# The cross-attention block's input fed a second time, transposed: centred Wq and rstd as the scale of the exponential in place of transposes of x

## The reference, cut to what matters

```python
def layernorm(x): return (x - mean(x)) / sqrt(var(x) + 1e-5)          # over D = 256
# x: (2, 1024, 256); context: (2, 64, 256); 16 heads of 64; 8 experts, top 2, F = 1024
q = layernorm(x) @ Wq;  k = context @ Wk * 64**-0.5;  v = context @ Wv
attn = softmax(q k^T);  x = x + tanh(g_xattn) * ((attn v) @ Wo + bo)
seq = layernorm(x).mean(axis=1);  probs = softmax(seq @ gate_w)       # top 2 experts per batch
x = x + tanh(g_ffn) * sum_e share_e * (gelu(layernorm(x) @ w1[e] + b1[e]) @ w2[e] + b2[e])
```

## Time and profile before

| | |
|---|---|
| median of 3 runs | 323.07 us (323.06 to 323.4) |
| the profiled execution | 322.94 us, of which the span of its instructions is 320.8 us |
| busy | PE 314.4, DVE 233.7, ACT 164.1, POOL 78.8 us |
| attention steps 0 to 16 | about 17 to 131 us of the span |

### The profile page before, as it was taken

How to read it: one execution, slowest core, us unless ns; L and a number is a source line. 1 busy time by engine, 2 the same in 40 slices (tenths; PEclk the granted TensorE clock), 3 DMA queues, 4 the chain that set the end, 5 groups by cost and what they waited for, 6 DMA issues and landing times.

```text
span 320.8 us, 5745 instructions
## 1 busy us (share of the span) xinstructions
PE 314.4 (98%) x1881; PEld 272.1 (85%) x1881; DVE 233.7 (73%) x563; ACT 164.1 (51%) x577; POOL 78.8 (25%) x158
## 2 busy tenths in 40 slices
PE   7899999999999999999999999999999999999996
PEld 7887988988999999988788888888887899888896
DVE  1889997978889999999998475466667554442643
ACT  2548555686766668775466254444533442321320
POOL 1325448484455536335600000000000000000000
PEclk9999999999999999999999999999999999999999
DMA  6992000000000017600007250000020000000011
GB/s 224 395 197 4 2 3 0 0 3 3 0 0 3 0 52 246 230 1 0 2 0 263 55 208 1 0 0 0 8 102 24 2 0 2 0 0 0 2 65 65
DMA packets 20765, 17.35 MB, mean 54 GB/s; under 512 B 11068, under 2 KB 16900, under 8 KB 20612
## 3 DMA queue, kind: packets, MB, share of 16 engines
q1 hardware_dynamic: 20464, 16.51, 17.0%
q10 hardware_dynamic: 276, 0.52, 0.5%
HBM read 14.93 MB, written 2.10 MB: 53 GB/s over the span
## 4 chain that ended last, share of the span: by engine, by line
PE 88%; DVE 7%; DMA 2%; issue 1%; ACT 1%; SPq 0%; DVEq 0%
PE ps L1098 26%; PE ps L1100 26%; PE ps L1099 26%; PE ps L1183 4%; DMA xt<-in_x_dram 2%; PE ps L1272 1%; PE ps L1118 1%; DVE mx L850 1%; PE ps L1156 1%; DVE pT_lo L808 1%; PE ps L1214 1%; PE ps L1370 1%; ACT sx L580 1%; DVE stats L729 1%; DVE sm L819 1%
## 5 line engine op out<-in xcount | busy, mean ns | idle before, releaser
L667 ACT ACTIVATE gel<-ps,b1sel 128x512 f32<-128x512 f32 x64 | 43.9, 690 | 95.5 <-PE ps L1100 95.4
L1057 DVE CAST h_hi<-gel 128x512 fp32r<-128x512 f32 x64 | 28.4, 443 | 58.7 <-ACT gel L667 58.5
L580 ACT ACTIVATE sx<-ps,mx 128x64 f32<-128x64 f32 x128 | 38.3, 327 | 27.6 <-DVE mx L850 27.6
L1098 PE MATMUL ps<-yT_hi,w_hi 128*128 128x512 f32 (+1 forms) x128 | 50.5, 395 | 0.0
L1099 PE MATMUL ps<-yT_lo,w_hi 128*128 128x512 f32 (+1 forms) x128 | 50.0, 390 | 0.0
L1100 PE MATMUL ps<-yT_hi,w_lo 128*128 128x512 f32 (+1 forms) x128 | 49.9, 390 | 0.0
L1059 DVE TENSOR_TENSOR h_lo<-gel,h_hi 128x512 fp32r<-128x512 f32 x64 | 44.9, 702 | 2.2
L466 POOL TENSOR_TENSOR sx<-sx,rs 128x512 f32<-128x512 f32 x32 | 33.2, 1058 | 48.0 <-DVE rs L824 47.8
L1098 PE MATMUL ps<-h_hi,w_hi 128*128 128x512 f32 x96 | 38.4, 400 | 0.0
L1100 PE MATMUL ps<-h_hi,w_lo 128*128 128x512 f32 x96 | 37.5, 390 | 0.0
L1099 PE MATMUL ps<-h_lo,w_hi 128*128 128x512 f32 x96 | 37.4, 390 | 0.0
(11 more groups left out here) (145 smaller groups left out, 672.7 us busy)
## 6 DMA issues: line engine op xcount, KB each, us to landing
stage_w<-in_L_ffn_w_dram SPq DMA_DIRECT2D x7, 1024.0 KB, 7.3
out_dram<-xt SPq DMA_DIRECT2D x6, 256.0 KB, 2.5
wqT<-in_L_xattn_Wq_dram SPq DMA_DIRECT2D x2, 512.0 KB, 7.9
wv_sb<-in_L_xattn_Wv_dram SPq DMA_DIRECT2D x2, 512.0 KB, 9.3
wo_sb<-in_L_xattn_Wo_dram SPq DMA_DIRECT2D x1, 1024.0 KB, 13.7
xt<-in_x_dram SPq DMA_DIRECT2D x1, 1024.0 KB, 10.7
stage_w<-in_L_ffn_w_dram SPq DMA_DIRECT2D x2, 512.0 KB, 4.4
wk_sb<-in_L_xattn_Wk_dram ACTq DMA_DIRECT2D x1, 512.0 KB, 4.2
```

Of the source, the lines that this page charges most:

```text
L580: last = nc.scalar.activation(sx[:, par, c0:c0 + M], ps[:, 2 * par + 1, c0 - BANK:c0 - BANK + M], ACT.Exp, bias=mx[:, par, h:h + 1], accum ...
L667: nc.scalar.activation(gel[:, f % 4, :], ps[:, h_bank, :], ACT.Gelu, bias=b1sel[:, b, slot, f:f + 1]).then_inc(gelu_done, 1)
L1057: nc.vector.tensor_copy(h_hi[:, f % 4, :], gel[:, f % 4, :]).then_inc(hhi_ready, 1)
L1098: mm(acc, hi_w, hi_x, start=start, stop=False)
```

## The change

The launch gets x a second time, laid out on the host as `xT` (partition = feature). Scores are now made from the raw transposed x. The mean is taken out by centring Wq over the feature axis (its row sums are removed on the chip before `score_pair`), and rstd is applied as the scale of the exponential, with the maxima of the last eight heads multiplied by it (`mxs`).

```diff
@@ SP: the loads
+            def load_xT(i):
+                t0, t1 = XT_LOADS[i]
+                part = 0 if t0 < XS0 else 1 if t0 < XS1 else 2
+                base = (0, XS0, XS1)[part]
+                sp.dma_start(xs[part][:, t0 - base:t1 - base, :, :], xT[:, t0:t1, :, :]).then_inc(ld_xT[i], 16)
...
-            load_x(1, 0, 2, TB // 2)
...
+            load_x(0, 0, 0, TB // 2)
+            load_xT(0)
...
+            sp.wait_ge(grp_done, number[("kT", 1)] + 1)
+            load_xT(2)
+            load_xT(3)
@@ POOL
-                t = s + LEAD
-                if active(t) and t != X_BY_DVE:
...
-                    nc.gpsimd.tensor_tensor(xn[:, par, :], tile, mean1[:, ds(t, 1)].broadcast_to([P, D]),
-                                            ALU.subtract).then_inc(xc_ready, 1)
...
-                if s == 1:
-                    newton(*X_PARTS[1], rstd1, ve_x, 2)
-                    pool.sem_inc(x_rstd, 1)
-                if s == 4:
-                    newton(*X_PARTS[2], rstd1, ve_x, 3)
-            pool.wait_ge(guess_ready, 1)
+                if active(s + LEAD):
+                    x_low(s + LEAD)
+                if s in (-1, 3, 6):
+                    x_rstds((-1, 3, 6).index(s))
...
+            def x_low(t):
+
+                pool.wait_ge(xhi_ready, t + 1)
+                nc.gpsimd.tensor_tensor(xT_lo[:, t % XB, :, :], x_raw(t), as_f32(xT_hi[:, t % XB, :, :]),
+                                        ALU.subtract).then_inc(xlo_ready, 1)
+
+            for half in range(2):
+                pool.wait_ge(wq_mean, half + 1)
+                for m in range(4 * half + 2, 4 * half + 4):
+                    last = nc.gpsimd.tensor_tensor(wqT[:, m, :], wqT[:, m, :], wq_off[:, m:m + 1].broadcast_to([P, D]), ALU.add)
+                last.then_inc(wq_pool, 1)
@@ ACT
+            def wq_centred(half):
+
+                act.wait_ge(wq_mean, half + 1)
+                for m in range(4 * half, 4 * half + 2):
+                    last = nc.scalar.activation(wqT[:, m, :], wqT[:, m, :], ACT.Identity, bias=wq_off[:, m:m + 1])
+                last.then_inc(wq_act, 1)
 
             group("kT", 0)
+            wq_centred(0)
             group("kT", 1)
+            wq_centred(1)
...
-                act.wait_ge(max_done, t + 1)
+                act.wait_ge(mxs_ready, t + 1)
...
-                                                ACT.Exp, bias=mx[:, par, h:h + 1],
+                                                ACT.Exp, bias=mxs[:, par, h - H // 2:h - H // 2 + 1],
+                                                scale=rstd1[:, t:t + 1],
@@ DVE
+            def wq_means(half):
+
+                blocks = slice(4 * half, 4 * half + 4)
+                dve.wait_ge(ld_wq[half], 16)
+                nc.vector.tensor_reduce(wq_off[:, blocks], wqT[:, blocks, :], AX, ALU.add).then_inc(wq_sum, 1)
+                dve.wait_ge(wq_sum, half + 1)
+                nc.vector.tensor_scalar(wq_off[:, blocks], wq_off[:, blocks], -1.0 / D, None, ALU.mult).then_inc(wq_mean, 1)
...
-            x_norm(0)
+            for half in range(2):
+                wq_means(half)
+            x_stats(0, range(0, TB // 2))
...
+            for g in A0[:4]:
                 group(*g)
-            x_low(0)
-            for g in A0[6:]:
+            x_norm(0)
+            for g in A0[4:]:
                 group(*g)
...
-                if s == 4:
-                    x_norm(2)
...
+                    dve.wait_ge(x_rstd, next(i for i, (t0, t1) in enumerate(X_PARTS) if t < t1) + 1)
+                    nc.vector.tensor_scalar(mxs[:, par, :], mx[:, par, H // 2:H], rstd1[:, t:t + 1], None,
+                                            ALU.mult).then_inc(mxs_ready, 1)
...
-                    x_norm(1)
...
-                if s in (2, 3):
-                    x_stats(3, range(TB + 4 * (s - 2), TB + 4 * (s - 2) + 4))
+                if s == 2:
+                    x_stats(1, range(TB // 2, TB))
+                    x_norm(1)
+                if s in (3, 4):
+                    x_stats(2, range(TB + 4 * (s - 3), TB + 4 * (s - 3) + 4))
+                if s == 5:
+                    x_norm(2)
@@ PE
-                pe.wait_ge(ld_wq[half], 16)
+                pe.wait_ge(wq_act, half + 1)
+                pe.wait_ge(wq_pool, half + 1)
...
-                    for k in range(KD):
-                        last = nc.tensor.transpose(ps[:, 7, k * P:(k + 1) * P], xn[:, q, k * P:(k + 1) * P], ident[:, :])
-                    last.then_inc(xT_done, 1)
```

More of the change, by code:

```diff
@@ L75, in gated_cross_attention_moe_kernel @@
     mx = place("mx", [P, 2, H])
+    mxs = place("mxs", [P, 2, H // 2])
     sm = place("sm", [P, 2, H])
@@ L114, in gated_cross_attention_moe_kernel @@
     ctxT = place("ctxT", [P, KD, P], at=first)
+    XS0, XS1 = 6, 14
+    xs = [place("xs0", [P, XS0, KD, P], at=first),
+          place("xs1", [P, XS1 - XS0, KD, P], at=[cursor[0]])]
     first2 = [cursor[0]]
@@ L138, in gated_cross_attention_moe_kernel @@
     pT_lo = place("pT_lo", [P, 2, NP, P], f32r, at=second)
-    xT_hi = place("xT_hi", [P, 2, KD, P], f32r, at=second)
-    xT_lo = place("xT_lo", [P, 2, KD, P], f32r, at=second)
-    xn = place("xn", [P, 2, D], at=second)
+    XB = 3
+    xT_hi = place("xT_hi", [P, XB, KD, P], f32r, at=second)
+    xT_lo = place("xT_lo", [P, XB, KD, P], f32r, at=second)
     yT_hi = place("yT_hi", [P, KD, NT * P], f32r, at=second)
@@ L169, in gated_cross_attention_moe_kernel @@
         ld_wk = [sem(f"ld_wk_{i}") for i in range(2)]
-        ld_x = [sem(f"ld_x_{i}") for i in range(4)]
+        ld_x = [sem(f"ld_x_{i}") for i in range(3)]
         ld_g, ld_bo, ld_gate, ld_b12 = sem("ld_g"), sem("ld_bo"), sem("ld_gate"), sem("ld_b12")
@@ L182, in gated_cross_attention_moe_kernel @@
         ln_ready, xc_ready = sem("ln_ready"), sem("xc_ready")
[L183 to L184 removed]
+        xhi_ready, xlo_ready = (sem(n) for n in ("xhi_ready", "xlo_ready"))
+        ld_xT = [sem(f"ld_xT_{i}") for i in range(4)]
+        wq_sum, wq_mean, wq_act, wq_pool = (sem(n) for n in ("wq_sum", "wq_mean", "wq_act", "wq_pool"))
+        mxs_ready = sem("mxs_ready")
         scores_done, head_done, max_done, sub_done, exp_done, sum_done, recip_done, mul_done = (
@@ L329, in gated_cross_attention_moe_kernel, with x_raw, wait_x_raw @@
         X_PARTS = [(0, TB // 2), (TB // 2, TB), (TB, NT)]
-        X_BY_DVE = X_PARTS[1][0]
+        XT_LOADS = [(0, 2), (2, XS0), (XS0, XS1), (XS1, NT)]
+        def x_raw(t):
+            part = 0 if t < XS0 else 1 if t < XS1 else 2
+            return xs[part][:, t - (0, XS0, XS1)[part], :, :]
+        def wait_x_raw(eng, t):
+            eng.wait_ge(ld_xT[next(i for i, (t0, t1) in enumerate(XT_LOADS) if t < t1)], 16)
         def run_steps(step):
@@ L833, in step @@
                         group(*g)
-                t = s + 1
-                if active(t) and t >= 2:
-                    q = (par + 1) % 2
-                    if s in Y_WITH_X:
-                        dve.wait_ge(yhi_ready, Y_WITH_X[s] + 1)
-                    dve.wait_ge(xhi_ready, t + 1)
-                    nc.vector.tensor_tensor(xT_lo[:, q, :, :], ps[:, 7, 0:D].rearrange("p (k i) -> p k i", k=KD),
-                                            as_f32(xT_hi[:, q, :, :]), ALU.subtract).then_inc(xlo_ready, 1)
                 if s in Y_WITH_X:
@@ L1431, in _laid_out @@
         a = a.T.reshape(-1, 128, a.shape[0]).transpose(1, 0, 2)
+    if name == "xT":
+        b, s, d = a.shape
+        a = a.reshape(b, 128, s // 128, d // 128, 128).transpose(4, 0, 2, 3, 1)
+        a = a.reshape(128, b * s // 128, d // 128, 128)
     return _np.ascontiguousarray(a)
```

96 lines of the change are left out of this document (39 added, 57 removed).

## The result

The changed kernel takes 341.87 us in the median (340.89 to 342.61, four runs) against 323.06 us (322.88 to 323.4) before: ratio 1.058, 95% interval 1.0549 to 1.0609. I had said 323.7 and at most 325.2. The profiled execution took 340.89 us, its span is 339.0. The granted clock of TensorE is 1.0 in both profiled executions, so the 18.2 us between their spans have to be found in waits and lengths. Single executions in a slower state of the chip are left out of all medians and ratios.

The account below looks back on a forecast made before the run. PE was taken to bound the kernel from about step 5 on, DVE and ACT before that. +1.9 us (POOL's new wait) - 1.3 us (steps 9 to 14) = +0.6 us on a median of 323.07 gave 323.7 us, range 322.1 to 325.2.

Parts of the forecast that it names:

- steps 1 to 6: Early attention steps, paced by DVE and ACT: one xT_lo (0.28 us) less, mxs (0.2 us) more, rounds nearly alike.
- Transposes: PE, steps 1 to 14: one pair of xn transposes less per step, 0.22 us each, at most 3.1 us.
- Steps 9 to 14: PE sets the pace again; six pairs of xn transposes less give -1.3 us.
- The start: Before the first scores: centring Wq makes PE start A one us later; mx(0) at 20.9 us, +0.4 us.
- The clock rival: The start: PE's gap before A halves its clock, 1.5 us more, late Wq another us; 324.7 to 326.2 us, chance 0.13.
- recip(5) at 61.8: DVE's reciprocal of tile 5, 61.74 us before, comes at 61.8, between 61.2 and 63.0.
- scores(8) at 75.1: PE's score matmul of step 8 begins at 75.1 us instead of 73.24, +1.9 us.
- POOL's new wait: Steps 6 to 8: two Newton blocks of 3.87 us in a row delay mul(6), and PE waits; +1.9 us.
- the first rival: Transposes pay in full, POOL's blocks not holding up mul(6): -1.6 to -2.8 us, 320.3 to 321.5 us; chance 0.12.
- The sum: Whole kernel: +1.9 - 1.3 = +0.6 us, predicting 323.7 us.
- The second rival: Half is hidden, recip(5) coming a us or more earlier: -0.3 to -1.1 us, 322.0 to 322.9 us; chance 0.15.

Follow-up runs that it names:

- e4_before_scale: The kernel before with a column of ones added as scale in the nine exponentials of a step; 332.28 us (1.0287).
- e3_neither: The changed kernel without the scale operand in the exponentials and without the product of the maxima (`mxs`); 324.74 us (1.0047).
- e1_no_scale: The changed kernel with the scale operand taken out of the exponentials, the product of the maxima kept; 332.47 us (1.028).
- e2_no_mxs: The changed kernel without the product of the maxima, the exponentials taking the unscaled maxima as bias; 331.40 us (1.0254).
- e7_act_mxs: The changed kernel with the product of the maxima made by ACT instead of DVE, ahead of the exponentials; 335.87 us (1.0379).
- e8_no_max: The changed kernel with the maxima left out of the softmax, two exponentials of 128x512 with scale per step; 324.22 us (1.0044).
- e5_neither_newton5: e3_neither with the third rstd (Newton) block on POOL moved from step 6 to step 5; 320.47 us (0.9916).

## Why the prediction was wrong

The step that failed is the one on steps 1 to 6, "So rounds of before and after are nearly alike", in two terms. The product of the maxima stood there "above a whole xT_lo of 0.28; I take 0.2": it takes 0.69 us in the mean, and without it 10.5 us come back. The scale of the exponentials was not costed at all, though it is an operand added to nine instructions per step, eight of which stand one behind the other on the loop: 9.4 us come back without it. I had drawn the loop rightly, and had named, as what would make me wrong, that DVE and ACT become the pace from step 9 on; but I gave it no chance and no price. The margin was thin, and I had not worked it out: PE's rounds were 6.95 us. Those of ACT and DVE follow only from `e4_before_scale`, where they set the pace at 7.6 to 7.7 us: 7.65 - 0.83 = 6.8 us, so that some 0.2 us more per round was enough. The Trainium skill, in ScalarE: Activation LUTs, under "What ACT_TABLE_LOAD costs", puts each operand with one value per partition (a pointer operand) at about 93 ns more. The traces nearly agree: exponentials 81 to 83 ns longer, whose starts lie 95 ns further apart. By the page's figure nine operands are 0.84 us per round, an estimate, beside the 0.83 measured.

The other steps, read in the run with neither (`e3_neither`), where PE sets the pace as I had assumed:

- *Transposes.* 0.22 us for a pair. Rounds of 6.72, 6.72, 6.77 and 6.74 us behind scores(8), where the kernel before has 6.95, 6.92, 6.95 and 6.95: right. In the changed kernel itself they are removed and bring nothing.
- *Steps 9 to 14, -1.3 us.* From scores(8) to scores(15) 123.03 - 75.46 = 47.57 against 122.16 - 73.24 = 48.92 us: -1.35, right.
- *The start, mx(0) at 20.9.* It came at 21.45 in the changed kernel and 21.8 here: +0.95 to +1.3 instead of +0.4. In the changed kernel DVE's sums started at 8.22 and A at 11.05, half a us before my 11.6; what I had too short was the way from there, where two operations of the guess take 0.60 and 0.66 us beside POOL's `xT_lo`:

```profile
15.59 0.16 DVE L758 TENSOR_SCALAR ve_x<-ve_x 128x4 f32<-128x4 f32 x1
15.63 1.42 POOL L500 TENSOR_TENSOR xT_lo<-xs,xT_hi 128x256 fp32r<-128x256 f32 x2 [3.40 <-ACT xT_hi L588]
...
15.79 0.60 DVE L759 SCALAR_TENSOR_TENSOR ve_x<-dm,ve_x 128x4 f32<-128x4 f32 x1
16.42 0.66 DVE L761 TENSOR_SCALAR rstd<-ve_x 128x4 int32<-128x4 int32 x1
```

  That is the same hold as for the product, at a second place. In `e3_neither`, where that `xT_lo` stands elsewhere, the two take 0.16 and 0.17 us; there A starts 0.26 us later and is slow, for the reason of the next point.
- *The clock rival.* Right as an event, and too dear. In the eleven profiled kernels that centre Wq, PE stood for 1.22 to 2.04 us ahead of A. In four of them, the changed kernel among them (1.41 us; the others 1.22 to 1.47), the granted clock stayed at 1.00. In the other seven (1.58 to 2.04 us) it was at 0.50, the 1.2 GHz of my rival, for some 3 us inside A, and A took 5.47 us instead of 4.35. `e3_neither` is one of them (2.04 us); its row of the granted clock:

```profile
PEclk9799999999999999999999999999999999999999
```

  The price is small, because DVE's splits of A had to be waited for anyhow: mx(0) comes at 21.45 to 21.60 us in those without the fall and at 21.46 to 22.28 in those with it (of the kernels that still take maxima), so 0 to 0.8 us, where I had put 1.5. The same fall came in step 8 behind the wait for POOL in `e1_no_scale`, `e2_no_mxs`, `e7_act_mxs` and `e8_no_max` (2.02 to 2.07 us), and not in `e3_neither` (2.02); it makes the two rounds there 1.3 us longer together.
- *recip(5) at 61.8, scores(8) at 75.1.* 61.81 and 75.46 here: right, recip(5) in part by luck, since mx(0) came 0.9 us later than I had counted and the steps up to 5 took that up. In the changed kernel 69.19 and 82.83.
- *POOL's new wait.* The two blocks stand in a row in every run that has them, and PE waits 2.0 us for the multiply here (1.86 in the changed kernel). Right as an event. Its price against the kernel before (+1.9 us at scores(8), measured +2.2) I had right for a PE-paced kernel, and in the changed kernel it is zero. Without it `e5_neither_newton5` came to 320.47 us, inside the 320.3 to 321.5 that the first rival gave. PE's timeline of this run at step 8:

```profile
73.79 0.66 PE L1217 MATMUL ps<-ident,sx 128*128 128x128 f32 x4 [2.02 <-POOL sx L485]
...
75.46 0.47 PE L1129 MATMUL ps<-a_hi,xT_hi 128*128 128x512 f32 x1
```

- *The sum.* 323.7 predicted for a kernel whose loop stays as it was; that kernel measures 324.74, and 323.46 in its one execution at the full clock. Of the miss of 18.2 us 17.1 are the two terms of the loop; the last 1.0 is of the size of the clock's falls. (The second rival's upper end should read 322.8, 323.07 less 0.3.)

What is open: `e3_neither` scattered by 2.6 us over its ten runs, where the kernel before scatters by a few tenths. The mean granted clock of each is on record: 323.46 us at 1.0; two of 323.17 and 323.41 and six of 324.49 to 324.94 at 0.995; 325.76 at 0.989. The profiled one, 323.41, has its one fall at the start. That the six have theirs behind the stall, where it costs 1.3 us, and the last has both, would fit; where the clock fell in executions without a trace, nothing shows.

## What to carry to other kernels

Where two loops run within a few per cent of each other (here about 6.8 and 6.95 us), price every operand and every small instruction that goes into the shorter one, times its count per round, before counting what leaves the longer one; a gain on PE is worth nothing once the other loop is the pace. A small instruction of VectorE on SBUF, in either of the two forms tried here, that is started by the same event as a long one of GpSimd can cost the rest of that long one: give it to ScalarE, or to another moment (tried here: ScalarE). And a stall has no price of its own: the same one was worth some 3 us with PE as the pace and nothing in the changed kernel, so a fix has to be tried where its loop is the one that binds. And read the granted clock of every profiled run ahead of its rounds: two rounds that looked like a longer stall were the same stall and a stretch at half the clock.

## What the runs showed of the hardware that I had not expected

A VectorE product of 128x8 took 166 to 1039 ns, its end falling within 0.04 us behind that of GpSimd's 128x512 multiply in twelve of sixteen executions, in both the tensor-scalar and the two-tensor form; on ScalarE it took 298 to 303 ns beside the same multiplies. The maxima, which read PSUM, kept their length beside the same multiplies (1.16 to 1.23 us). A scale operand of one value per partition made an exponential of 128x64 81 to 83 ns longer, and one of 128x512 72 ns (755 against 683); with a column of ones it was the same (408 ns for 128x64). A wait of 1.58 to 2.04 us ahead of A was followed by some 3 us at a granted clock of 0.50 in seven kernels, one of 1.22 to 1.47 us by none in four; later in the kernel a wait of 2.02 us was followed by such a stretch in one kernel and by none in another.
